# Graph network stack on one core: the order of VectorE's sums in the upper triangle, and the place of the near-diagonal step

## The chip, the cores and the metric

The kernel runs on one core of a Trainium2 chip. The metric is the device time of one execution in microseconds (us). Before the change it was 1927.98, the median of three runs (1926.94 to 1928.78).

## The reference

Four graph layers run one after the other over the same matrix `adj` (8192 x 8192, fp32) and the states `x` (8192 x 64):

```
h = relu(layernorm(x)); x = x + adj @ dropout(h, u)
h = relu(layernorm(x)); x = x + l2norm(relu(concat(h, (adj @ h + h) / (rowsum(adj) + 1)) @ W + b))
h = relu(layernorm(x)); x = x + (D^-1/2 (adj + I) D^-1/2 @ h) @ W      # D = rowsum(adj) + 1
h = relu(layernorm(x)); x = x + concat(h, adj @ h / (rowsum(adj) + 1)) @ W^T
```

Each layer needs one product of the whole matrix with 64 columns, and the row sums of `adj`. A layer's states of a row block exist only when that block's sum over all 8192 columns is done in the layer before.

## The kernel before

**Tiling.** The matrix is cut into 16 x 16 units of 512 x 512. A unit is one load of 1024 KB into one of 12 ring buffers; the diagonal units have two buffers of their own. "Row" means a block of 512 rows. With 64 columns of states as weights a matmul uses half of TensorE's array, and two of them on different halves run side by side; a unit is 4 source tiles of 128 x 512, in fp32 (8 matmul records of one line in the profile).

**Stages.** The matrix doesn't fit in the core's memory, so it is streamed. A first pass (to about 790 us) does layer 0 and the part of layer 1 below the diagonal, and VectorE sums the rows there. The second pass takes the rows from high to low (the upper triangle): a unit there serves layer 1 and layer 2 at once, if the source row's states of both layers are known. It is written in `PAIRS`, two rows at a time: pair 0 is rows (10, 9), pair 1 (8, 7), pair 2 (6, 5), pair 3 (4, 3), pair 4 (2, 1). Row 0 is done in between ("cover") and behind. Then come a head of rows 0 to 3, rows 4 to 15 for layers 2 and 3, and a last stage of single units for layer 3.

**Fours.** In a pair, 2 rows x 2 source rows x 2 layers would be 8 unit products. `four_even` and `four_odd` do them in 7, from combinations of units made by VectorE, each an operation of 128 x 2048:
- `first_form` (L1261): a21 + a22 into `first_sum`, two buffers in turn. It waits for the loads and for the four before last to have used that buffer.
- `third_form` (L1271): a11 - a21 in place of a21.
- `last_forms` (L1281, L1285): first_sum - a11 in place of a11, once TensorE has used a11 in its P1 (`first_taken`); then a12 less this in place of a12, once TensorE has used a12 in its P2 (`second_taken`).

An even four is four steps on TensorE: P2 with P1 (L828, L830), P5 with P4 (L842, L844; needs the first form), P7 with P6 (L852, L854; needs L1281), and P1 of the next four with P3 (L865, L868; needs L1285). An odd four is three: P2 with P4 (L883, L885), P5 with P6 (L890, L892; needs L1281), P7 with P3 (L898, L900; needs L1285).

**The order of a pair** is written out in `PAIR_STEPS`: two covers, fours 0 and 1, the near-diagonal step, four 2, four 3 and plain steps, where pair 1 has fours 0 to 2 only, pair 2 has its one plain step last, and pairs 3 and 4 have plain steps 7 and 6 between fours 2 and 3. Behind the first cover TensorE forms Z (L720) for the higher row of the pair before, behind four 0's first step for the lower one. `near_diagonal` (L905 to L922) multiplies the pair's own near unit for layer 1, and the near unit of the pair before, loaded again, for layer 2 ("behind"); for that it needs the layer-2 states of the higher row of the pair before, and that row is ended by `end_layer_1` on VectorE. `plain_both` (L924) takes one source row for both layers and both rows; the last plain step of a pair needs the layer-2 states of the lower row of the pair before.

**Queues.** Each engine follows its own list in order. SP issues the loads in the order of `loads_in_order`; a load into a ring buffer waits until the unit 12 places before is freed by TensorE, counted in the order of `units_let_go`. VectorE's list for the pairs is the loop at L1487. ScalarE copies P1, makes the square roots of the layer norms and copies the transposed states (`copy_hT`), in an order of its own, in which the copy for row 0 stands between the roots of rows 4 and 3.

Of the kernel before, what the change touches and what calls it, by code (L numbers as in the profile page):

```python
# [205 lines left out]
def gnn_stack(nc, x_in, u_in, stream_in, w1_in, b1_in, w2_in, w3_in, x_out):  # L206
# [6 lines left out]
    with ctx:  # L213
# [6 lines left out]
        def sem(name):  # L220
            return ctx.enter_context(nc.semaphore(name))
# [76 lines left out]
        out_stored = sem("out_stored")  # L298
        states_formed = sem("states_formed")
        late_states_formed = sem("late_states_formed")  # L300
        unit_formed = sem("unit_formed")
        first_taken = sem("first_taken")
        second_taken = sem("second_taken")
# [178 lines left out]
        def _(act):  # L482
# [124 lines left out]
                    if p == len(PAIRS) - 2 and b == PAIRS[p][0]:  # L607
                        copy_hT(1, 0)
            act.wait_ge(*fours_taken(FOURS_BEFORE[-1] - 1))
            act.wait_ge(unit_formed, 4 * FOURS_BEFORE[-1])  # L610
            for r in ADDED[:HEAD]:
                keep_diag(r)

# [50 lines left out]
        def _(pe):  # L664
# [155 lines left out]
            def four_even(p, i, after_first=None, after_second=None):  # L820

                (hi, lo), (s1, s2) = PAIRS[p], FOURS[p][i]
                n, last = FOURS_BEFORE[p] + i, i == len(FOURS[p]) - 1
                a11, a12, a21, a22 = [(2, b, g) for b in (hi, lo) for g in (s1, s2)]
                await_unit(a12, 1)
                await_unit(a11, 1)
                for k in range(TPR):
                    two = nc.tensor.matmul(product("P2"), h[1][:, s2 * TPR + k], source_tile(slot(a12), k),  # L828
                                           start=i == 0 and k == 0, stop=False)
                    one = nc.tensor.matmul(product("P1"), h[1][:, s1 * TPR + k], source_tile(slot(a11), k),  # L830
                                           start=i == 0 and k == 0, stop=i >= len(FOURS[p]) - 2 and k == TPR - 1)
                two.then_inc(second_taken, 1)
                one.then_inc(first_taken, 1)
                if after_first is not None:
                    after_first()
                if i == 0 and p > 0:
                    pe.wait_ge(pair_taken, 3 * p - 2)
                pe.wait_ge(*states_formed_of((s1, s2)))
                pe.wait_ge(unit_formed, 4 * n + 1)
                await_unit(a22, 2)  # L840
                for k in range(TPR):
                    five = nc.tensor.matmul(product("P5"), formed((s1, s2), 1)[:, k], source_tile(first_sum[n % 2], k),  # L842
                                            start=i == 0 and k == 0, stop=last and k == TPR - 1)
                    four = nc.tensor.matmul(product("P4"), formed((s1, s2), 4)[:, k], source_tile(slot(a22), k),  # L844
                                            start=i == 0 and k == 0, stop=False)
                five.then_inc(sum_taken, 1)
                four.then_inc(unit_freed, 1)
                if after_second is not None:
                    after_second()
                pe.wait_ge(unit_formed, 4 * n + 3)  # L850
                for k in range(TPR):
                    seven = nc.tensor.matmul(product("P7"), formed((s1, s2), 3)[:, k], source_tile(slot(a21), k),  # L852
                                             start=i == 0 and k == 0, stop=last and k == TPR - 1)
                    nc.tensor.matmul(product("P6"), formed((s1, s2), 2)[:, k], source_tile(slot(a11), k),  # L854
                                     start=i == 0 and k == 0, stop=last and k == TPR - 1)
                seven.then_inc(unit_freed, 1)
                pe.wait_ge(unit_formed, 4 * n + 4)
                if i == 0 and p > 0:
                    pe.wait_ge(pair_taken, 3 * p - 1)
                if not last:  # L860
                    t1, t2 = FOURS[p][i + 1]
                    await_unit((2, hi, t1), 1)
                for k in range(TPR):
                    if not last:
                        one = nc.tensor.matmul(product("P1 again"), h[1][:, t1 * TPR + k],  # L865
                                               source_tile(slot((2, hi, t1)), k), start=i == 0 and k == 0,
                                               stop=i >= len(FOURS[p]) - 3 and k == TPR - 1)
                    three = nc.tensor.matmul(product("P3"), h[0][:, s2 * TPR + k], source_tile(slot(a12), k),  # L868
                                             start=i == 0 and k == 0, stop=False)
                if not last:  # L870
                    one.then_inc(first_taken, 1)
                three.then_inc(unit_freed, 2)

            def four_odd(p, i):
# [10 lines left out]
                    nc.tensor.matmul(product("P4"), formed((s1, s2), 4)[:, k], source_tile(slot(a22), k),  # L885
                                     start=False, stop=False)
                two.then_inc(second_taken, 1)
                pe.wait_ge(unit_formed, 4 * n + 3)
                for k in range(TPR):
                    five = nc.tensor.matmul(product("P5"), formed((s1, s2), 1)[:, k], source_tile(first_sum[n % 2], k),  # L890
                                            start=False, stop=last and k == TPR - 1)
# [1 line left out]
                                           start=False, stop=last and k == TPR - 1)  # L893
                five.then_inc(sum_taken, 1)
                six.then_inc(unit_freed, 1)
                pe.wait_ge(unit_formed, 4 * n + 4)
                for k in range(TPR):
                    seven = nc.tensor.matmul(product("P7"), formed((s1, s2), 3)[:, k], source_tile(slot(a21), k),  # L898
                                             start=False, stop=last and k == TPR - 1)
# [135 lines left out]
            for p, (hi, lo) in enumerate(PAIRS):  # L1035
                for kind, n in PAIR_STEPS[p]:
# [4 lines left out]
                    elif kind == "four" and n == 0:  # L1041
                        if p == 0:
                            pe.wait_ge(*gathered(1, 11))
                            pe.wait_ge(part_copied, PARTS.index((2, 11)) + 1)
                        four_even(p, 0, after_first=(lambda: finish(1, PAIRS[p - 1][1])) if p else None,
                                  after_second=lambda: turn_own(1, hi))
                        turn_own(1, lo)
                    elif kind == "four" and n % 2 == 0:
                        four_even(p, n)
                        if p == len(PAIRS) - 1:  # L1050
                            turn_own(1, 0)
                    elif kind == "four":
                        four_odd(p, n)
                    elif kind == "near":
                        near_diagonal(p)
                    else:
                        plain_both(p, n)
            cover(COVER_AT_END[0])
            finish(1, PAIRS[-1][0])
# [94 lines left out]
        def _(dve):  # L1154
# [97 lines left out]
            def first_form(p, i):  # L1252
# [6 lines left out]
                if n >= 2:  # L1259
                    dve.wait_ge(*fours_taken(n - 2))  # L1260
                nc.vector.tensor_tensor(first_sum[n % 2][:, :], slot(a21)[:, :], slot(a22)[:, :],  # L1261
                                        ALU.add).then_inc(unit_formed, 1)
                dve.wait_ge(unit_formed, 4 * n + 1)

            def third_form(p, i):

# [3 lines left out]
                dve.wait_ge(*loaded(a11))  # L1270
                nc.vector.tensor_tensor(slot(a21)[:, :], slot(a11)[:, :], slot(a21)[:, :],  # L1271
                                        ALU.subtract).then_inc(unit_formed, 1)
                dve.wait_ge(unit_formed, 4 * n + 2)

            def last_forms(p, i):

# [3 lines left out]
                dve.wait_ge(first_taken, n + 1)  # L1280
                nc.vector.tensor_tensor(slot(a11)[:, :], first_sum[n % 2][:, :], slot(a11)[:, :],  # L1281
                                        ALU.subtract).then_inc(unit_formed, 1)
                dve.wait_ge(unit_formed, 4 * n + 3)
                dve.wait_ge(second_taken, n + 1)
                nc.vector.tensor_tensor(slot(a12)[:, :], slot(a12)[:, :], slot(a11)[:, :],  # L1285
                                        ALU.subtract).then_inc(unit_formed, 1)
                dve.wait_ge(unit_formed, 4 * n + 4)

            def combine_first_layer(p):

# [54 lines left out]
            def begin_layer_1(b):  # L1345
                scaled_z(1, b, deg_clipped_inverse)
# [137 lines left out]
                end_layer_1(b)  # L1484
            scale_own(1, 10)
            scale_own(1, 9)
            for p, (hi, lo) in enumerate(PAIRS):  # L1487
                if p > 0:
                    combine_first_layer(p - 1)
                    begin_layer_1(PAIRS[p - 1][0])  # L1490
                    combine_fifth(p - 1)
                first_form(p, 0)
                if p > 0:
                    combine_high(p - 1)
                third_form(p, 0)
                if p > 0:
                    combine_low(p - 1)
                last_forms(p, 0)
                first_form(p, 1)
                third_form(p, 1)  # L1500
                last_forms(p, 1)
                if p > 0:
                    end_layer_1(PAIRS[p - 1][0], begun=True)
                for n in range(FORMED_BY_GPSIMD, len(SOURCE_PAIRS)):
                    if p > 0 and SOURCE_PAIRS[n][1] == PAIRS[p - 1][0]:
                        form_states(n)
                for i in range(2, len(FOURS[p])):
                    first_form(p, i)
                    third_form(p, i)
                    if i == 2:  # L1510
                        add_behind(p - 1)
                        if p == len(PAIRS) - 1:
                            scale_own(1, 0)
                    last_forms(p, i)
                if p > 0:
                    end_layer_1(PAIRS[p - 1][1])
                if p < len(PAIRS) - 1:
                    for b in PAIRS[p + 1]:
                        scale_own(1, b)
            last = len(PAIRS) - 1  # L1520
            combine_first_layer(last)
            end_layer_1(PAIRS[-1][0])
# [59 lines left out]
```

## Time and profile before

| what | value |
|---|---|
| median of the runs | 1927.98 us (1926.94 to 1928.78) |
| profiled execution: its own time | 1928.73 us |
| its span, first to last instruction | 1926.8 us |
| mean granted TensorE clock | 0.998 |
| TensorE (PE) busy | 1870.4 us, 97% |
| VectorE (DVE) busy | 1065.3 us, 55% |
| ScalarE (ACT) busy | 111.9 us, 6% |
| moved by DMA | 675.63 MB, mean 351 GB/s |

The profile is of one execution; its own time is the span and what lies around it. Times in its views count from the span's start. An idle time in brackets is that of the engine just before an instruction, with what ended it. PEclk is the clock that TensorE was granted, 1.00 being 2.4 GHz.

### The profile page before, as it was taken

The page shows a single profiled execution, that of the slowest core. Times are in us where ns is not written, and L with a number is a line of the kernel's source. Part 1 is how long each engine was busy: PE and PEld are TensorE (multiplying, and loading weights), DVE is VectorE, ACT ScalarE, POOL GpSimd, SP SyncE. Part 2 cuts the span into 40 slices and gives each one's busy share as a digit, 9 for nine tenths or more (in the row PEclk, how much of TensorE's full clock was granted, in tenths as well). Part 3 has the DMA queues.
Part 4 walks back from the last instruction along what each step waited for, and adds up shares of the span by engine and source line. Part 5 has one row for each costly group of instructions (what it writes and reads, how often), then busy time and mean ns, then how long its engine had stood idle before and what let it go on. Part 6 is the DMA issues. An engine that isn't in the chain of part 4 may idle for free.

```text
span 1926.8 us, 19280 instructions
## 1 busy us (share of the span) xinstructions
PE 1870.4 (97%) x7784; PEld 697.8 (36%) x7784; DVE 1065.3 (55%) x1156; ACT 111.9 (6%) x288; POOL 9.6 (0%) x26
## 2 busy tenths in 40 slices
PE   5899999999999999999999999999999999999998
PEld 1233333333333333333333333344444444344343
DVE  8988899999887762867875745321111100110322
ACT  0000000000000001100000001111100000000000
POOL 0000000000000000100000000000000000000000
PEclk9999999999999999999999999999999999999999
DMA  9999999999988884588778787497999889999998
GB/s 386 421 421 421 421 421 421 421 421 411 351 329 321 294 304 172 231 330 355 292 296 323 287 334 278 191 399 288 400 380 366 343 307 422 376 358 415 355 422 341
DMA packets 95894, 675.63 MB, mean 351 GB/s; under 512 B 11200, under 2 KB 13248, under 8 KB 14272
## 3 DMA queue, kind: packets, MB, share of 16 engines
q1 hardware_dynamic: 92880, 672.18, 87.1%
q10 hardware_dynamic: 2928, 2.23, 0.3%
q8 instruction: 63, 1.03, 0.2%
q14 instruction: 23, 0.19, 0.0%
HBM read 672.27 MB, written 2.10 MB: 350 GB/s over the span
## 4 chain that ended last, share of the span: by engine, by line
PE 85%; DMA 8%; DVE 5%; issue 1%; ACT 0%; SPq 0%; DVEq 0%
PE acc L666 43%; PE acc L696 23%; DMA ring<-stream_in 8%; PE Z L720 3%; PE HT L666 2%; PE acc L931 2%; PE DEG L943 2%; PE acc L828 2%; PE acc L852 1%; PE acc L842 1%; PE acc L865 1%; PE acc L883 1%; DVE ring L1285 1%; PE DEG L731 1%; PE DEG L915 1%
## 5 line engine op out<-in xcount | busy, mean ns | idle before, releaser
L666 PE MATMUL acc<-ring,states 128*64 128x512 f32 x3992 | 894.3, 596 | 33.7 <-DMA ring<-stream_in 27.4
L666 PEld LDWEIGHTS acc<-ring,states 128*64 128x64 f32 x3992 | 281.5, 137 | 586.6 <-issue 555.6
L696 PE MATMUL acc<-ring,states 128*128 128x512 f32 x1032 | 453.2, 596 | 2.0 <-DVE states L1225 2.0
L1380 DVE TENSOR_TENSOR row_sum<-row_sum,ring 128x2048 f32<-128x2048 f32 x194 | 444.6, 2292 | 18.5 <-DMA ring<-stream_in 13.5
L696 PEld LDWEIGHTS acc<-ring,states 128*128 128x128 f32 x1032 | 193.5, 191 | 245.1 <-issue 245.1
L1217 DVE TENSOR_TENSOR z_sb<-Z,deg_rsqrt 128x256 f32<-128x256 f32 x16 | 6.8, 424 | 335.3 <-PE Z L720 335.2
L666 PE MATMUL acc<-diag,states 128*64 128x512 f32 x432 | 103.6, 595 | 0.6 <-DMA diag<-stream_in 0.6
L1441 DVE TENSOR_TENSOR y<-acc,y 64x512 f32<-64x512 f32 x36 | 24.6, 683 | 110.8 <-PE acc L666 110.5
L720 PEld LDWEIGHTS Z<-below,y 128*128 128x128 f32 x512 | 62.5, 191 | 51.9 <-issue 18.0
L720 PE MATMUL Z<-below,y 128*128 128x64 f32 x512 | 70.0, 280 | 2.2 <-DVE y L1442 2.2
L1407 DVE TENSOR_TENSOR diag<-diag,ident 128x384 f32<-128x384 f32 x12 | 6.7, 559 | 108.4 <-ACT row_sum L533 108.4
L514 ACT COPY y<-acc 64x512 f32<-64x512 f32 x34 | 19.8, 581 | 748.6 <-PE acc L666 739.9
L1285 DVE TENSOR_TENSOR ring<-ring 128x2048 f32<-128x2048 f32 x17 | 39.0, 2292 | 42.6 <-PE acc L883 42.3
L666 PEld LDWEIGHTS acc<-diag,states 128*64 128x64 f32 x432 | 31.3, 137 | 65.6 <-issue 63.6
L931 PE MATMUL acc<-ring,states 128*64 128x512 f32 x88 | 41.4, 615 | 5.5 <-DVE states L1225 5.5
L666 PE MATMUL HT<-ring,states 128*64 128x512 f32 x168 | 42.6, 595 | 0.0
L1233 DVE TENSOR_TENSOR x<-Z,x 128x256 f32<-128x256 f32 x16 | 6.8, 424 | 63.6 <-PE Z L720 63.3
L933 PE MATMUL acc<-ring,states 128*64 128x512 f32 x88 | 41.5, 616 | 0.0
L1380 DVE TENSOR_TENSOR row_sum<-ring 128x2048 f32<-128x2048 f32 x16 | 36.7, 2292 | 6.7 <-DMA ring<-stream_in 5.8
L943 PE MATMUL DEG<-ring,states 128*64 128x512 f32 x88 | 39.6, 593 | 0.0
L941 PE MATMUL acc<-ring,states 128*64 128x512 f32 x88 | 39.6, 592 | 0.0
L1271 DVE TENSOR_TENSOR ring<-ring 128x2048 f32<-128x2048 f32 x17 | 39.0, 2292 | 0.6
(157 smaller groups left out, 1295.6 us busy)
## 6 DMA issues: line engine op xcount, KB each, us to landing
ring<-stream_in SPq DMA_DIRECT2D x609, 1024.0 KB, 10.3
diag<-stream_in SPq DMA_DIRECT2D x28, 1024.0 KB, 11.6
x<-x_in SPq DMA_DIRECT2D x4, 512.0 KB, 6.7
y<-u_in SPq DMA_DIRECT2D x4, 512.0 KB, 8.5
x_out<-x ACTq DMA_DIRECT2D x16, 128.0 KB, 7.0
below<-w_in ACTq DMA_DIRECT2D x6, 16.0 KB, 5.7
bias<-b_in ACTq DMA_DIRECT2D x1, 32.0 KB, 9.8
```

Of the source, the lines that this page charges most:

```text
L666: return nc.tensor.matmul(half_of(bank, half), h[layer % 2][:, J], moving, start=start, stop=stop)
L696: done = nc.tensor.matmul(acc[bank][:, :], states[:, J * 2 * F:(J + 1) * 2 * F], source_tile(slot(key), k), start=first and k == 0, stop=l ...
L720: mm_z = nc.tensor.matmul(Z[:, t * F:(t + 1) * F], own_y(b)[:, t * P:(t + 1) * P], below[:, layer, :], start=True, stop=True)
L828: two = nc.tensor.matmul(product("P2"), h[1][:, s2 * TPR + k], source_tile(slot(a12), k), start=i == 0 and k == 0, stop=False)
L931: nc.tensor.matmul(product("P2"), h[1][:, J], source_tile(slot((2, hi, g)), k), start=False, stop=last and k == TPR - 1)
L933: done = nc.tensor.matmul(product("P3"), h[0][:, J], source_tile(slot((2, hi, g)), k), start=False, stop=last and k == TPR - 1)
L941: nc.tensor.matmul(product("P4"), h[1][:, J], source_tile(slot((2, lo, g)), k), start=False, stop=last and k == TPR - 1)
L943: done = nc.tensor.matmul(product("plain"), h[0][:, J], source_tile(slot((2, lo, g)), k), start=g == PLAIN[p][0] and k == 0, stop=last and ...
L1271: nc.vector.tensor_tensor(slot(a21)[:, :], slot(a11)[:, :], slot(a21)[:, :], ALU.subtract).then_inc(unit_formed, 1)
L1285: nc.vector.tensor_tensor(slot(a12)[:, :], slot(a12)[:, :], slot(a11)[:, :], ALU.subtract).then_inc(unit_formed, 1)
L1380: nc.vector.tensor_tensor(row_sum[:, :], before, slot(key)[:, :], ALU.add).then_inc(unit_summed, 1 if count > 1 else 2)
L1441: chain(nc.vector.tensor_tensor(own_y(r, 0), half_of(bank, 0), own_y(r, 0), ALU.add))
```

## The change

A semaphore of its own, `sum_formed`, now counts the first forms, so these may be made out of turn; `unit_formed` counts the other three of each four. For pairs 1 to 4 VectorE makes the first and third form of four 0 ahead of combining the pair before, and the first form of four 2 ahead of `last_forms(p, 1)`. In pairs 3 and 4 the lower row of the pair before is ended ahead of four 3's forms. On TensorE the near-diagonal step of pairs 1 to 4 is issued inside four 2, behind its first step, and no longer ahead of it. The order of the loads, the order in which units are counted free, and row 0's own steps are as they were. All calls of `wait_ge` on `unit_formed` go from 4 a four to 3 a four; these are left out below but for two.

```diff
+        sum_formed = sem("sum_formed")
@@ four_even
-                pe.wait_ge(unit_formed, 4 * n + 1)
+                pe.wait_ge(sum_formed, n + 1)
                 await_unit(a22, 2)
...
-                pe.wait_ge(unit_formed, 4 * n + 3)
+                pe.wait_ge(unit_formed, 3 * n + 2)
@@ the steps of a pair on TensorE
                     elif kind == "four" and n % 2 == 0:
-                        four_even(p, n)
+                        four_even(p, n, after_first=lambda: near_diagonal(p))
...
-                    elif kind == "near":
+                    elif kind == "near" and p == 0:
                         near_diagonal(p)
-                    else:
+                    elif kind == "plain":
                         plain_both(p, n)
@@ first_form
-                                        ALU.add).then_inc(unit_formed, 1)
-                dve.wait_ge(unit_formed, 4 * n + 1)
+                                        ALU.add).then_inc(sum_formed, 1)
+                dve.wait_ge(sum_formed, n + 1)
@@ the pairs on VectorE
-            for p, (hi, lo) in enumerate(PAIRS):
-                if p > 0:
-                    combine_first_layer(p - 1)
-                    begin_layer_1(PAIRS[p - 1][0])
-                    combine_fifth(p - 1)
+            first_form(0, 0)
+            third_form(0, 0)
+            last_forms(0, 0)
+            first_form(0, 1)
+            third_form(0, 1)
+            last_forms(0, 1)
+            for p, (before_hi, before_lo) in enumerate(PAIRS[:-1], 1):
+                for b in PAIRS[p]:
+                    scale_own(1, b)
                 first_form(p, 0)
-                if p > 0:
-                    combine_high(p - 1)
                 third_form(p, 0)
-                if p > 0:
-                    combine_low(p - 1)
+                combine_first_layer(p - 1)
+                begin_layer_1(before_hi)
+                combine_fifth(p - 1)
+                combine_high(p - 1)
+                combine_low(p - 1)
                 last_forms(p, 0)
                 first_form(p, 1)
                 third_form(p, 1)
+                first_form(p, 2)
                 last_forms(p, 1)
-                if p > 0:
-                    end_layer_1(PAIRS[p - 1][0], begun=True)
+                end_layer_1(before_hi, begun=True)
                 for n in range(FORMED_BY_GPSIMD, len(SOURCE_PAIRS)):
-                    if p > 0 and SOURCE_PAIRS[n][1] == PAIRS[p - 1][0]:
+                    if SOURCE_PAIRS[n][1] == before_hi:
                         form_states(n)
-                for i in range(2, len(FOURS[p])):
-                    first_form(p, i)
-                    third_form(p, i)
-                    if i == 2:
-                        add_behind(p - 1)
-                        if p == len(PAIRS) - 1:
-                            scale_own(1, 0)
-                    last_forms(p, i)
-                if p > 0:
-                    end_layer_1(PAIRS[p - 1][1])
-                if p < len(PAIRS) - 1:
-                    for b in PAIRS[p + 1]:
-                        scale_own(1, b)
+                third_form(p, 2)
+                last_forms(p, 2)
+                add_behind(p - 1)
+                if p == len(PAIRS) - 1:
+                    scale_own(1, 0)
+                if ("plain", 7) in PAIR_STEPS[p][:-1]:
+                    end_layer_1(before_lo)
+                if len(FOURS[p]) == 4:
+                    first_form(p, 3)
+                    third_form(p, 3)
+                    last_forms(p, 3)
+                if ("plain", 7) not in PAIR_STEPS[p][:-1]:
+                    end_layer_1(before_lo)
```

## Rows read from the trace of the kernel before

**Rows 1.** The page, part 1: busy, instructions; part 5: busy, mean ns | idle before, releaser.
```profile
PE 1870.4 (97%) x7784; PEld 697.8 (36%) x7784; DVE 1065.3 (55%) x1156; ACT 111.9 (6%) x288; POOL 9.6 (0%) x26
...
L696 PE MATMUL acc<-ring,states 128*128 128x512 f32 x1032 | 453.2, 596 | 2.0 <-DVE states L1225 2.0
```
**Rows 2.** Waits of PE, 843 to 1215 us: in total, times, longest.
```profile
PE DEG L915 <- DVE states L1225: 7.5, 4, 1.9
PE acc L931 <- DVE states L1225: 5.5, 3, 2.2
```
**Rows 3.** Timeline of PE: start, us, engine, line; idle before in brackets.
```profile
898.17 0.61 PE L931 MATMUL acc<-ring,states 128*64 128x512 f32 x1 [1.13 <-DVE states L1225]
...
971.36 0.61 PE L931 MATMUL acc<-ring,states 128*64 128x512 f32 x1 [2.19 <-DVE states L1225]
...
1005.77 0.59 PE L890 MATMUL acc<-row_sum,diag 128*64 128x512 f32 x1
...
1012.21 0.59 PE L898 MATMUL acc<-ring,diag 128*64 128x512 f32 x1
...
1014.68 0.61 PE L915 MATMUL DEG<-ring,states 128*64 128x512 f32 x1 [1.87 <-DVE states L1225]
...
1058.29 0.99 PE L931 MATMUL acc<-ring,states 128*64 128x512 f32 x1 [2.19 <-DVE states L1225]
...
1187.09 5.37 PE L696 MATMUL acc<-ring,states 128*128 128x512 f32 x8 [1.95 <-DVE states L1225]
```
**Rows 4.** Timeline of DVE in the pairs, same columns.
```profile
856.12 0.68 DVE L1322 TENSOR_TENSOR y<-DEG,pair_sums 64x512 f32<-64x512 f32 x1 [0.32 <-PE Z L720]
...
881.27 2.29 DVE L1261 TENSOR_TENSOR row_sum<-ring 128x2048 f32<-128x2048 f32 x1
...
885.93 0.68 DVE L1330 TENSOR_TENSOR y<-DEG,y 64x512 f32<-64x512 f32 x1
...
891.51 0.42 DVE L1217 TENSOR_TENSOR z_sb<-Z,deg_clipped_inverse 128x256 f32<-128x256 f32 x1
...
897.60 0.42 DVE L1225 SCALAR_TENSOR_TENSOR states<-centred,inverse 128x256 f32<-128x256 f32 x1
...
978.50 0.68 DVE L1294 TENSOR_TENSOR y<-acc,y 64x512 f32<-64x512 f32 x1 [6.49 <-PE DEG L943]
...
998.83 2.29 DVE L1271 TENSOR_TENSOR ring<-ring 128x2048 f32<-128x2048 f32 x1
1002.09 2.29 DVE L1281 TENSOR_TENSOR ring<-row_sum,ring 128x2048 f32<-128x2048 f32 x1 [0.97 <-PE acc L865]
1006.05 2.29 DVE L1285 TENSOR_TENSOR ring<-ring 128x2048 f32<-128x2048 f32 x1 [1.66 <-PE acc L883]
...
1014.00 0.42 DVE L1225 SCALAR_TENSOR_TENSOR states<-centred,inverse 128x256 f32<-128x256 f32 x1
...
1067.13 0.68 DVE L1294 TENSOR_TENSOR y<-acc,y 64x512 f32<-64x512 f32 x1 [8.19 <-PE DEG L943]
```
**Rows 5.** Timeline of ACT in pair 4, same columns.
```profile
1121.10 0.74 ACT L521 COPY y<-HT 64x256 f32<-64x256 f32 x2 [18.91 <-PE HT L763]
```
**Rows 6.** SP's loads: the one issued at 877.8, then the one at 883.3.
```profile
DMA to landing us min/median/max: 4.8/4.8/4.8
...
DMA to landing us min/median/max: 10.7/10.7/10.7
```
**Rows 7.** A window in pair 3: us, PE busy, PEclk, DMA share, GB/s.
```profile
1059.00:1060.00 1.00, 1.00 (x6) 0.50 1.12 475
```
**Rows 8.** Windows ahead of and in the last stage, same columns.
```profile
1790.00:1800.00 10.00, 10.00 (x44) 1.00 0.71 233
...
1870.00:1880.00 10.00, 10.00 (x54) 1.00 1.02 425
```
**Rows 9.** Waits of PE, then of SP, from 1215 us on.
```profile
PE acc L666 <- DMA ring<-stream_in: 1.3, 3, 0.6
...
SPq L432 <- PE acc L696: 314.2, 102, 4.2
```

## What the change will do

> **What bounds the kernel now.** I read the page first: TensorE is busy 97% of the span [rows 1], so only its idle time, its clock and its own work can move the end. Then its waits in the stretch of pairs 1 to 4: four waits of the near-diagonal step (L915) and three of a plain step (L931), all on a state that VectorE writes at L1225 [rows 2]. Then the timelines, to see what stands ahead of those states.
>
> The idle time in that view runs from the modelled end of a matmul. Matmuls of one half last 0.59 and start 0.43 apart (15 starts lie between the first L890 at 1005.77 and the last L898 at 1012.21, 6.44 / 15) [rows 3], so a wait costs 0.16 more than its idle time. In pair 3 the last L898 starts at 1012.21, the next step was due at 1012.64 and starts at 1014.68: 2.04 lost for 1.87 idle. The four near-diagonal waits (7.5 idle, about 1.87 each) are worth 2.04 each; the plain ones 1.29 in pair 1 (idle 1.13), 2.35 in pair 2 and 2.35 in pair 3 (idle 2.19 both).
>
> The one in pair 3 costs more. Behind it the granted clock is 0.50, the 1.2 GHz level [rows 7]. From the state's end to the first combine, with one plain step on TensorE between them, VectorE idles 8.19 there and 6.49 behind the equal wait of pair 2 [rows 4]: the low clock cost 1.70. The wait before 1187.09, in row 0's steps behind the pairs, has the same sequel: eight matmuls take 5.37 [rows 3], where 8 x 453.2 / 1032 = 3.51 is usual [rows 1]. The change doesn't touch that wait.
>
> **The change, part by part.**
>
> *Near-diagonal step behind the third four's first step.* The state it waits for ends a chain in pair 3 of L1281 at 1002.09, L1285 at 1006.05 (held by the second four's first step), the end of layer 1, and L1225, which ends at 1014.42 [rows 4]. The third four's first step needs neither that state nor a sum, only loaded units and layer-1 states. It takes eight starts of 0.43, 3.43 in all, so the near step comes due at 1012.64 + 3.43 = 1016.07, 1.4 after the state is ready. All four waits go. What could be late next is the third step of that four, which needs L1281: with its sum made before, VectorE does L1271 and L1281 in 2 x 2.33 behind the state (two such forms take 4.66 from 881.27 to 885.93, [rows 4]), ready at about 1019.1, and TensorE asks for it two more steps on, at 1022.9. Spare 3.8.
>
> The two near-diagonal units come free one step later, and SP takes loads in order, so everything behind them may be issued 3.43 later. In pair 2's case the load that waits for the freed unit was issued at 883.3 and took 10.7 to land, at 894.0, where the one issued at 877.8 took 4.8 [rows 6]; it was mostly queued, and up to 5 of delay vanishes in that queue. VectorE asks for it only after the state at 898.02. I take 0; the ends are 0 and 3.43 a pair.
>
> *First and third forms ahead of combining.* These are 2 x 2.33 = 4.66 of VectorE work moved in front of the pair's end, where it idles 6.49 (pair 2's end) and 8.19 (pair 3's) [rows 4]; pair 1's forms have no layer end in their way. They fit with 1.8 to spare. Behind the pair's end nothing gets earlier by it: combine_low waits for Z until 856.12 in pair 1 [rows 4], after which come L1281 and L1285 as now. So this part gains 0 by itself and costs 0. If the cover is gone, each us beyond the spare delays the first combine; TensorE has one cover step of 3.51 [rows 1] before it needs the third of these adds (3 x 0.72 = 2.2, 0.68 each in [rows 4] and 0.04 to the next), so 1.3 more is free.
>
> *The third four's sum ahead of last_forms(p, 1).* L1271 starts at 998.83, the sum would run from 1001.16, L1281 from 1003.49 to 1005.78 in place of 1002.09 to 1004.38. Today VectorE is idle there, 0.97 before L1281 and 1.66 before L1285 [rows 4], 2.63 together, so the sum's 2.33 fits and L1285 still starts at 1006.05: the state is no later. But TensorE's second step of the second four starts at 1005.77 [rows 3], and from VectorE's end to a matmul's start it takes 0.15 (898.02 to 898.17) to 0.26 (1014.42 to 1014.68). It would start at 1005.93 to 1006.04: a new wait of 0.16 to 0.27, in all four pairs. No trace shows this wait itself; bounded below by 0 (a hidden start) and above by the next smallest wait of this kind, 1.29. The instants are known to 0.01, so I take 0.2, 0.8 in all.
>
> *End of the lower row.* Pair 1: behind its new states VectorE starts L1271 at 881.27 in place of the sum, does three forms (6.99) and L1330 (0.72) by 888.98, then the layer's end, 6.51 from 891.51 to 898.02: state at 895.49, TensorE at 895.64. TensorE would be ready at 898.17 - 1.29 - 2.04 + 0.2 = 895.04. The plain step starts at 895.64 and 0.6 of its wait stays: the gain of pair 1, near step and new wait included, is 2.53.
> Pair 2: the layer's end stays behind the fourth four's last form, which waits for that four's first step. Both engines keep their distance from there, and the 2.35 stays. Gain 2.04 - 0.2 = 1.84.
> Pair 3: the layer's end now lies under the third four and two plain steps (4 x 3.43 = 13.7), so the 2.35 and the 1.70 of low clock go. Gain 1.84 + 2.35 + 1.70 = 5.89.
> Pair 4: no plain wait today. The layer's end asks ScalarE for a root, behind its copy of row 0's turned states, which starts at 1121.10 and takes 0.74, after the third four [rows 5]. VectorE stops there until about 1121.9, then needs 4.5 to the state and 3 x 2.33 for the fourth four's forms: 1133.4 by today's times. TensorE asks for them two plain steps and one more behind about 1121.0, at 1138.1. Spare 4.7, cost 0. Gain 1.84.
>
> **Sum.** 2.53 + 1.84 + 5.89 + 1.84 = 12.10. Of this 10.4 is idle time and 1.70 is clock. The profiled execution took 1928.73 (span 1926.8 and 1.93 around it), 0.75 over the median of the runs; since the sum holds a clock loss seen in it, I take it from its own time: 1928.73 - 12.10 = 1916.6. Does it reach the end? Loads behind the pairs are issued when TensorE frees units (SP waits 314.2 for L696 after 1215), TensorE waits for DMA 1.3 in all [rows 9], and just ahead of the last stage the DMA share falls to 0.71 [rows 8], so the ring is full when that stage starts and its loads shift with TensorE.
>
> **The rivals.**
>
> *The clock falls elsewhere.* Of two equal waits of 2.19 [rows 3] one was followed by a fall, the other not. Pair 2's wait stays and may cost 1.70; row 0's may not: 1918.3 or 1914.9, both at once give no difference. The Trainium skill (TensorE: Matmul & The Clock Gate, Part 1) says that the observation runs freely and is not tied to the program, which would make this a matter of chance in each execution; by it 1918.3 is as fair as 1916.6, and the two equal waits with different sequels agree.
>
> *The pairs' ends keep their waits*, because VectorE is late with something the timelines hide (the root behind the copy, add_behind waiting for the later near step). Then pair 3 keeps its 4.05 and pair 1 its 0.7: 1921.4. Against it: the spares of 3.8 and 4.7.
>
> *Given back in the last stage.* There the DMA share is 1.02 [rows 8]; if it sets the pace from before row 0's steps, nothing is left: 1928.7. Against it: the 0.71 ahead of that stage and the short DMA waits [rows 8, 9].
>
> *Slower: combining waits behind the hoisted forms.* If the loads of a pair's first four landed only at the pair's end, both forms would run behind it: 4.66 less 1.3 free, 3.36 in four pairs, 13.4 against 12.1 gained. From 0.7 later than that it is measurably slower: 1932.8. It decides only if the loads come much later than now; pair 2's landed at 894.0, before VectorE can ask.
>
> **How the numbers follow.** 0.56 for the forecast, 0.20 for the clock, 0.10 for the kept waits, 0.09 for given back, 0.05 for slower. Low end: no new wait (0.8), no fall behind row 0's wait (1.7) and the 0.75 to the median: 1913.3, widened to 1912.8. High end: kept waits, 1921.4, widened to 1921.8; new waits near their upper bound would reach it too. Beyond that lie the last two cases, 0.14. A measurement tells 0.2% (3.9 us) from no change: faster 0.86, same 0.09, slower 0.05.
>
> **What would show it.** L915 has no wait, L890 four short ones near 0.05 to 0.1 idle, L931 one below 0.6 in pair 1 and one near 2.2 in pair 2, none in pair 3; the wait behind 1166 stands some 12 us earlier. VectorE shows L1261 and L1271 before the first combine. Wrong would be: waits of L720 or L842 at a pair's start, L890 waits over 0.5, or DMA waits of TensorE near the end.

## The result and the profile after

The changed kernel takes 1918.49 us (median of 4 runs, 1917.7 to 1920.65) against 1927.46 (4 runs) for the kernel before: ratio 0.9949, 95% interval 0.9936 to 0.9961, 9.0 us faster. The profiled execution took 1920.65, span 1918.7, which is 8.1 under the 1928.73 of the profiled execution before. The forecast was 1916.6, a gain of 12.1.

The page of the changed kernel, part 1 (the lines of code named here are one higher than before):

```profile
PE 1868.0 (97%) x7784; PEld 692.7 (36%) x7784; DVE 1065.1 (56%) x1156; ACT 112.1 (6%) x288; POOL 9.6 (0%) x26
```

TensorE's waits in the changed kernel, 843 to 1215 us (total, times, longest). They answer to [rows 2]:

```profile
PE acc L866 <- issue: 3.0, 2, 1.8
PE acc L932 <- DVE states L1226: 2.8, 2, 2.2
PE acc L697 <- DVE states L1226: 2.0, 1, 2.0
```

The near-diagonal step (now L916) is gone from the list. Of the three plain waits two are left. New is L866, the fourth step of a four, whose releaser the view doesn't find. The timeline of PE shows where these are (idle time before in brackets, [rows 3] before):

```profile
896.56 0.61 PE L932 MATMUL acc<-ring,states 128*64 128x512 f32 x1 [0.56 <-DVE states L1226]
...
967.78 0.95 PE L932 MATMUL acc<-ring,states 128*64 128x512 f32 x1 [2.21 <-DVE states L1226]
...
1026.60 0.61 PE L866 MATMUL acc<-ring,states 128*64 128x512 f32 x1 [1.83 <-issue]
...
1110.56 0.61 PE L866 MATMUL acc<-ring,states 128*64 128x512 f32 x1 [1.21 <-issue]
...
1180.61 3.67 PE L697 MATMUL acc<-ring,states 128*128 128x512 f32 x8 [1.95 <-DVE states L1226]
```

The waits of 0.56 and 2.21 in pairs 1 and 2 are as forecast. Behind the second the clock fell (first matmul 0.95 long); behind the last, row 0's, it did not: 3.67 for eight matmuls where before it was 5.37. L866 multiplies the first unit of the next four's higher row, in pair 3 unit (4, 9), in pair 4 unit (2, 9). SP's view of the loads of these two, in the changed kernel:

```profile
L433 SPq DMA_DIRECT2D ring<-stream_in x1: 327/327/327, 1017.9 to 1017.9; - x1
...
DMA to landing us min/median/max: 8.6/8.6/8.6
...
L433 SPq DMA_DIRECT2D ring<-stream_in x1: 328/328/328, 1102.5 to 1102.5; - x1
...
DMA to landing us min/median/max: 8.0/8.0/8.0
```

1017.9 + 8.6 = 1026.5, and TensorE starts at 1026.60; 1102.5 + 8.0 = 1110.5, and it starts at 1110.56. "issue" hid a DMA. The load of the same unit in pair 3 before the change, by SP's view:

```profile
L432 SPq DMA_DIRECT2D ring<-stream_in x1: 328/328/328, 1018.3 to 1018.3; - x1
...
DMA to landing us min/median/max: 9.3/9.3/9.3
```

and the timeline of PE:

```profile
1028.44 0.59 PE L865 MATMUL acc<-ring,states 128*64 128x512 f32 x1
```

It landed at 1027.6 and was read at 1028.44: 0.8 spare. What changed is the distance from the issue, when the near step frees the buffer, to the read. Before, three steps of TensorE lay between them, 10.1 (1018.3 to 1028.44). In the changed kernel there are two: the read was due at 1024.6 (1026.60 less the 1.83 idle and 0.16), 6.7 behind the issue at 1017.9. The load took 0.7 less there (8.6 for 9.3), so one step of 3.43 less the spare of 0.8 and this 0.7 is a loss of 1.9, as measured.

In pair 4 the load of (2, 9) took 9.2 from 1107.0 before and was read at 1117.06, a spare of 0.9. It took 1.2 less in the changed kernel (8.0), which gives a loss of 1.3; measured are 1.21 idle and 0.16.

Cutting the span at each start of combining gives a time for each pair. VectorE's first combine, before:

```profile
843.49 0.68 DVE L1294 TENSOR_TENSOR y<-acc,y 64x512 f32<-64x512 f32 x1 [11.44 <-PE DEG L943]
905.31 0.68 DVE L1294 TENSOR_TENSOR y<-acc,y 64x512 f32<-64x512 f32 x1 [6.49 <-PE DEG L943]
...
1165.97 0.68 DVE L1294 TENSOR_TENSOR y<-acc,y 64x512 f32<-64x512 f32 x1 [18.66 <-PE DEG L943]
```

and after:

```profile
844.49 0.68 DVE L1295 TENSOR_TENSOR y<-acc,y 64x512 f32<-64x512 f32 x1 [6.71 <-PE DEG L944]
903.77 0.68 DVE L1295 TENSOR_TENSOR y<-acc,y 64x512 f32<-64x512 f32 x1 [2.03 <-PE DEG L944]
976.69 0.68 DVE L1295 TENSOR_TENSOR y<-acc,y 64x512 f32<-64x512 f32 x1 [3.73 <-PE DEG L944]
1061.28 0.68 DVE L1295 TENSOR_TENSOR y<-acc,y 64x512 f32<-64x512 f32 x1 [6.17 <-PE DEG L944]
1159.49 0.68 DVE L1295 TENSOR_TENSOR y<-acc,y 64x512 f32<-64x512 f32 x1 [25.20 <-PE DEG L944]
```

The idle times show the forms made ahead: 11.44 becomes 6.71. The table has the differences of such rows for every kernel of this study (e8 to e10 are second profiles); a star marks a pair that holds a fall of the clock, 1.70 long.

| kernel | pair 1 | pair 2 | pair 3 | pair 4 | start to pair 1 | behind pair 4 |
|---|---|---|---|---|---|---|
| before | 61.82 | 73.19 | 88.63* | 98.84 | 843.49 | 760.8* |
| e8, before again | 61.82 | 74.89* | 88.62* | 98.84 | 844.83 | 760.7* |
| after | 59.28 | 72.92* | 84.59 | 98.21 | 844.49 | 759.2 |
| e0, after again | 59.28 | 72.92* | 84.70 | 98.20 | 844.59 | 758.8 |
| e1 | 62.53 | 74.88* | 84.52 | 98.77 | 844.12 | 759.2 |
| e2 | 61.61 | 72.25 | 86.11 | 98.02 | 843.87 | 759.2 |
| e3 | 59.28 | 71.23 | 82.53 | 96.79 | 843.55 | 758.3 |
| e9, e3 again | 59.29 | 72.93* | 82.54 | 96.78 | 843.84 | 760.4* |
| e4 | 61.83 | 73.18 | 84.52 | 98.84 | 843.38 | 758.6 |
| e5 | 61.82 | 73.18 | 88.61* | 98.77 | 843.60 | 760.4* |
| e6 | 58.57 | 68.80 | 82.53 | 96.79 | 845.21 | 761.1* |
| e10, e6 again | 58.57 | 68.80 | 82.53 | 96.79 | 844.14 | 760.5* |
| e7 | 59.28 | 71.22 | 82.54 | 96.85 | 843.62 | 760.4* |

The column "start to pair 1" is the start of combining itself, counted from the span's start. Between executions of one kernel a pair repeats within about 0.1 apart from the falls, while the unchanged part ahead of pair 1 varies by 1.3 (843.49 and 844.83 in the kernel before).

### The profile page after: what moved, and what is told of

Same layout as the page of the kernel before. It is cut to its first block, busy times and chain, and to the rows that moved or that the text cites. A ratio compares the mean times of both kernels' runs of the same rounds, so it can differ in the third digit from the quotient of the medians.

```text
span 1918.7 us, 19280 instructions
## 1 busy us (share of the span) xinstructions
PE 1868.0 (97%) x7784; PEld 692.7 (36%) x7784; DVE 1065.1 (56%) x1156; ACT 112.1 (6%) x288; POOL 9.6 (0%) x26
## 4 chain that ended last, share of the span: by engine, by line
PE 89%; DMA 7%; DVE 3%; issue 1%; SPq 0%; ACT 0%; DVEq 0%
PE acc L667 44%; PE acc L697 23%; DMA ring<-stream_in 7%; PE Z L721 3%; PE HT L667 2%; PE acc L932 2%; PE DEG L944 2%; PE acc L829 2%; PE acc L843 2%; PE acc L853 1%; PE acc L866 1%; PE acc L884 1%; PE acc L899 1%; PE acc L891 1%; PE DEG L732 1%; PE DEG L916 1%
```

## The experiments

All were timed beside the kernel before (4 to 11 runs of each kernel), apart from the three second profiles. The median of the kernel before on those chips was 1928.5 to 1928.9.

**e0, the changed kernel again.** 

> The changed kernel as it is, beside the others on one chip. 1918.5 (9.0 under before). TensorE's first P1 matmul of four 3 (inside four 2) waits 1.8 in pair 3 and 1.2 in pair 4, as in the first profile.

1919.85, ratio 0.9952 (0.9939 to 0.9964). The L866 waits are there again, 1.94 and 1.19.

**e1, the near step put back; e3, one load moved.** Two theories on L866: the load came late, because SP could issue it only when the near step had freed its buffer; or a form of VectorE held it.

```diff
# e1
-                        four_even(p, n, after_first=lambda: near_diagonal(p))
+                        four_even(p, n)
...
-                    elif kind == "near" and p == 0:
+                    elif kind == "near":
# e3, in step_loads and in units_let_go
+        if p >= 3 and n == 3:
+            return [(2, hi, s1), (2, lo, s1), (2, lo, s2), (2, hi, s2)]
...
-            at = PLACE[2, lo, s1]
+            at = min(PLACE[2, lo, s1], PLACE[2, hi, s1])
```

> The changed kernel with the near-diagonal step put back ahead of four 2; VectorE's order stays changed. Theory (loads): the waits of P1 in pairs 3 and 4 come from the load of four 3's unit (4, 9) or (2, 9), which SP can't issue before the near step has freed its units; with the near step ahead they vanish (3.4 won), the four near waits of 2.04 return (8.2 lost), pair 1's plain wait vanishes (0.7 won): 4.1 over the changed kernel, about 1922.6, less 1.7 where the clock falls once less. Rival (forms): those waits are for VectorE, whose order changed, and then they stay: about 1926.

> The changed kernel, with the load of four 3's first unit of the higher row issued ahead of the two of the lower row, in pairs 3 and 4 alone: two places earlier, where it waits for units that the second four frees. Theory (loads): it lands 5 us earlier, both waits of P1 go, 3.4 won: about 1915.1. Rival (forms): nothing moves, 1918.5. A second rival (DMA bandwidth): the lower row's loads land later in its place and VectorE's forms of four 3 hold TensorE, 1917 to 1919.

e3 takes 1914.27, ratio 0.9925 (0.9911 to 0.9938), and neither pair has a wait on L866's step. VectorE's order is that of the changed kernel, so the form theory falls, and the lower row's later loads cost nothing. In pair 3 the unit is issued at 1009.3, 35.2 behind the pair's start where it was 41.2 in the changed kernel's first profile. SP's loads in e3:

```profile
L435 SPq DMA_DIRECT2D ring<-stream_in x1: 430/430/430, 1009.3 to 1009.3; - x1
...
DMA to landing us min/median/max: 8.9/8.9/8.9
```

It lands at 1018.2. The step that reads it, in e3's timeline of PE, holds this matmul and no wait:

```profile
1021.97 0.59 PE L868 MATMUL acc<-ring,states 128*64 128x512 f32 x1
```

Against e0, pairs 3 and 4 are 2.17 and 1.41 shorter: 3.6 for the expected 3.4. The medians lie 5.6 apart, which is more. In the profiles the rest is falls of the clock and the part ahead of pair 1 (e9, the same kernel, took 1917.76 once); that the same holds for the other runs is not shown.

e1 takes 1925.33, ratio 0.9982 (0.9973 to 0.9991), where 1922.6 was expected. L866 waits no more, which agrees. But the near waits came back at 1.76 and pair 1 didn't win its 0.7: it lost 3.25 against after in place of the 1.3 expected there. Two waits of TensorE stand in pair 1 of e1:

```profile
880.22 0.61 PE L916 MATMUL DEG<-ring,states 128*64 128x512 f32 x1 [1.76 <-DVE states L1226]
899.44 0.61 PE L932 MATMUL acc<-ring,states 128*64 128x512 f32 x1 [1.84 <-DVE states L1226]
```

and VectorE, in e1, shows why the second is there:

```profile
881.84 2.29 DVE L1272 TENSOR_TENSOR ring<-ring 128x2048 f32<-128x2048 f32 x1
...
887.42 2.29 DVE L1282 TENSOR_TENSOR ring<-row_sum,ring 128x2048 f32<-128x2048 f32 x1 [3.29 <-PE acc L831]
```

L1282 waits 3.29 for the third four's first step, which with the near step ahead ends 3.4 later, and the sum's 2.33 taken out of VectorE's chain only makes this wait longer. So in pair 1 the early sum is worth something only when the near step stands behind.

**e2, only the near step moved; e4, only the lower row's end; e5, only the forms.** The kernel before with one part of the change each.

```diff
# e2
-                        four_even(p, n)
+                        four_even(p, n, after_first=lambda: near_diagonal(p))
# e4, ahead of the forms of four 3; from the end of pairs 3 and 4 it is taken away
+                    if i == 3 and p >= 3:
+                        end_layer_1(PAIRS[p - 1][1])
# e5: the changed kernel with e1's lines, and
                 third_form(p, 2)
-                last_forms(p, 2)
                 add_behind(p - 1)
...
+                last_forms(p, 2)
...
+                end_layer_1(before_lo)      # at the end of every pair, in place of both calls
```

> The kernel before, with nothing changed but the near-diagonal step, which stands behind four 2's first step. If the parts of the change were independent, it would win the 8.2 of the near waits less the 3.4 of the new load waits: 4.8, about 1922.7. Theory: in pair 1 VectorE's chain from the higher row's states over three forms and add_behind to the lower row's states is what bounds, and TensorE only waits longer at the plain step, so pair 1 wins nothing: 2.0 (pair 2) + 0.05 (pair 3) + 0.7 (pair 4) = 2.8, about 1924.7.

> The kernel before, with nothing changed but the place of the lower row's end in pairs 3 and 4, ahead of four 3's forms. Theory: pair 3's plain wait of 2.35 goes and nothing else, 1925.1, or 1923.4 where the clock fell behind that wait. The near waits (4 x 1.87 idle) stay. Rival: VectorE's stop at the root in pair 4 holds four 3's forms: slower than before.

> The kernel before, with nothing changed but the forms: first and third of four 0 ahead of combining, the sum of four 2 ahead of last_forms(p, 1). Theory: the near waits stay, and the sum's 2.33 leaves the chain from the higher to the lower row's states in pair 1, whose plain wait of 1.29 goes: 1926.2. The forms ahead of combining win 0. Rival: hoisting alone makes the states earlier, near waits shorter by 1 or more each: 1922 or less.

e2: 1925.34, ratio 0.9980 (0.9971 to 0.9989), 3.2 under before where the theory said 2.8 and independent parts 4.8. Pair 1 gives 0.2 in place of 2.5. The near waits are gone in it, and TensorE has these instead:

```profile
889.38 0.64 PE L852 MATMUL acc<-ring,diag 128*64 128x512 f32 x1 [0.90 <-DVE ring L1281]
898.34 0.61 PE L931 MATMUL acc<-ring,states 128*64 128x512 f32 x1 [1.88 <-DVE states L1225]
...
1026.82 0.61 PE L865 MATMUL acc<-ring,states 128*64 128x512 f32 x1 [1.05 <-DVE row_sum L1261]
```

Without the early sum L1281 comes 2.33 later, and VectorE's chain from the higher to the lower row's states sets the plain step. The third line is the load wait of pair 3: the view names L1261, but TensorE's step doesn't wait for this form, and by SP's view the load was issued at 1018.9 and took 7.8, so it landed at 1026.7. In pair 4 it is 0.76. So the near step alone brings the load waits, with VectorE's order as it was.

e4: 1923.14, ratio 0.9973 (0.9962 to 0.9984). Pair 3 is 4.11 shorter, the 2.41 of the wait and the 1.70 of the fall behind it; no other pair moves, and the stop at the root costs nothing. The medians lie 5.4 apart, 1.2 more than pair 3 gives; row 0's wait had no fall behind it in e4's profile and had one in both of the kernel before.

e5: 1928.63, ratio 1.0002 (0.9993 to 1.0011): nothing, where 1.3 was expected in pair 1. The forms alone gain 0, for the reason that e1 showed. In the kernel before, VectorE's timeline has the wait that decides it:

```profile
886.86 2.29 DVE L1281 TENSOR_TENSOR ring<-row_sum,ring 128x2048 f32<-128x2048 f32 x1 [0.25 <-PE acc L830]
```

In e5 this form (now L1282) waits 2.58 and starts at the same distance from the pair's start, 43.30 for 43.37.

By the medians the three alone give 3.2 + 5.4 - 0.1 = 8.4, with falls of the clock mixed in, and together 9.0. By the pairs, the stars taken off at 1.70 each, it is 2.8 + 2.4 + 0.1 = 5.3 against 7.5: the sum lacks 2.3 in pair 1 and 1.0 in pair 2, where the near step and the early sum need each other, and has 1.2 too much in pairs 3 and 4, where the load waits are longer in the whole change.

**e7, forms where they were.** The changed kernel with e3's load, but the first and third form of four 0 not ahead of combining:

```diff
-                first_form(p, 0)
-                third_form(p, 0)
                 combine_first_layer(p - 1)
                 begin_layer_1(before_hi)
                 combine_fifth(p - 1)
+                first_form(p, 0)
                 combine_high(p - 1)
+                third_form(p, 0)
                 combine_low(p - 1)
```

> The run with four 3's unit first, but the first and third form of four 0 made where they were before, among the steps of combining. Theory: they win nothing, since behind them combine_low waits for Z anyway: the same as that run, pairs of 59.3, 71.2, 82.5 and 96.8 from combine to combine. Rival (the hoist matters with the near step moved): pair's first steps wait for L1262 or the states come up to 4.7 later, and 1 to 2 a pair are lost, 1918 to 1922.

1915.63, ratio 0.9932 (0.9918 to 0.9945), an interval that overlaps with e3's, and the pairs are those of e3 within 0.06. This part wins nothing.

**e6, fewer waits.** e3's load, and VectorE's idle times around four 3 in pair 2 filled:

```diff
+                    if p == 2:
+                        begin_layer_1(before_lo)
+                        norm_asked(before_lo)       # bias, squares, sum, root asked
...
+                    last_forms(p, 3, between=(lambda: norm_taken(before_lo)) if p == 2 else None)
+                if p == 2:
+                    states_after_norm(before_lo)
# pair 1
+                if p == 1:
+                    end_layer_1(before_lo)
                 add_behind(p - 1)
```

> As the run with that unit first, and in pair 2 the lower row's layer end is begun in VectorE's idle times around four 3's L1282, and in pair 1 it stands ahead of add_behind. Theory: of the 6.5 of the layer end some 2.9 leave the chain behind L1286, so pair 2's wait of 2.35 goes, and pair 1's 0.7 too: 3.1 under the run before, about 1912.0, and no wait is left in the pairs behind which the clock could fall (up to 1.7 more in an execution where it fell there). Rival: the inserted small operations delay L1282 past TensorE's second step (0.4 spare) and the wait only moves to L891: about 1914 to 1915.

1912.37, ratio 0.9916 (0.9903 to 0.9930), 16.5 under before, the lowest median of all. The intervals of e6 and e3 overlap and the medians lie 1.9 apart, so the times alone don't tell the two; the pairs do: pair 1 is 0.71 and pair 2 2.43 shorter than in e3, 3.1 as expected, in both profiles of e6. In e6's window over all pairs TensorE has no idle time (us, PE busy, PEclk, DMA share, GB/s):

```profile
843.00:1170.00 327.00, 327.00 (x1432) 1.00 0.82 333
```

**e8 to e10, does the instant decide a fall?** In the first profiles of before, e4 and e5 the wait near 971 had no fall behind it, and those at 1058.3 and 1187.1 (before, e5) each had one.

> The kernel before, a second profile. Theory (the instant decides): TensorE's waits at 1058.3 and 1187.1 from the span's start are again followed by the clock at 0.50, that at 971.4 is not. Rival (chance in each execution): the fall stands behind other waits than in the first profile, or none.

> The kernel with four 3's unit first, a second profile. Theory (the instant decides): no fall behind the waits near 966.8 and 1174.5, as in its first profile. Rival (chance): a fall behind one of them in one of these looks.

> The kernel with fewer waits, a second profile. Theory (the instant decides): the one long wait left, near 1173.0, is again followed by a fall, eight matmuls of 5.37. Rival (chance): they may take 3.67.

e8 has a fall behind all three, also at 972.71. e9 has two where e3 had none. e10 has its one fall again (eight matmuls of 5.37), which both answers allow. In pair 2 of e9 it comes 1.3 into the plain step:

```profile
967.15 0.61 PE L934 MATMUL acc<-ring,states 128*64 128x512 f32 x1 [2.21 <-DVE states L1228]
...
968.47 1.06 PE L934 MATMUL acc<-ring,states 128*64 128x512 f32 x1
```

So which wait is followed by a fall differs between executions of one kernel. This doesn't settle the theory in its strict form, for in e8 and e9 the waits ended 0.3 to 3.0 later than in the first profiles (972.71 for 971.36), and where two kernels' waits ended at the same instant (before and e5 at 971.4, 1058.3 and 1187.1) the sequels were equal. Against it stands row 0's wait in two kernels, which ended 0.15 apart, with opposite sequels. In e3:

```profile
1174.49 3.67 PE L699 MATMUL acc<-ring,states 128*128 128x512 f32 x8 [1.94 <-DVE states L1228]
```

and in e7:

```profile
1174.64 5.37 PE L699 MATMUL acc<-ring,states 128*128 128x512 f32 x8 [1.95 <-DVE states L1228]
```

Chance in each execution fits all 13 profiles, but what decides a fall is not shown. Over all 13 profiles here a fall stands behind 15 of the 29 waits of 1.94 to 2.21 and behind none of the shorter ones in the pairs.

## Why the prediction was right or wrong

The measured time lies in the range, 1.9 over the value, on the side of the high end. That it is only 1.9 is in part luck. I subtracted the gain from the time of the profiled execution, 1928.73, which lies 1.3 over the median of the four runs before. Median against median the gain is 9.0 for 12.1, and profile against profile 8.1: 2.9 of idle time is missing, and the part ahead of pair 1, which the change doesn't touch, happened to take 1.0 more (844.49 for 843.49).

- *The four near waits go*: right, all four, and L1282 was in time. e2 confirms that the move alone does it; there a new wait of 0.90 for L1281 leaves 0.94 of the 2.04 in pair 2.
- *The new wait of L890*: too large. The timeline of DVE in pair 1 of the changed kernel:

```profile
869.40 2.29 DVE L1282 TENSOR_TENSOR ring<-row_totals,ring 128x2048 f32<-128x2048 f32 x1
```

and that of PE:

```profile
871.75 0.64 PE L891 MATMUL acc<-row_totals,diag 128*64 128x512 f32 x1
```

The step (now L891) starts 0.06 behind VectorE's end, and its first matmul lasts 0.64 in place of 0.59; no idle time shows. I had put 0.2 a pair; from the pair's start it begins at 27.26 and began at 27.27 (870.76) before, so at most the 0.05 of the longer matmul is lost, and 0.6 of the 0.8 never was.
- *Pair 1*: 2.53 forecast, 2.54 measured. *Pair 2*: 1.84 forecast, 1.97 measured with the fall taken off (73.19 less 72.92 - 1.70); its plain wait stays, 2.21 as said.
- *Pairs 3 and 4*: 5.89 and 1.84 forecast, 4.04 and 0.63 measured. This is the step that failed: "The two near-diagonal units come free one step later [...] I take 0; the ends are 0 and 3.43 a pair". I looked at one load, the one issued at 883.3 behind pair 1's near step; it brings a unit of pair 2's first four, which VectorE asks for only behind the state at 898.02. In pairs 3 and 4 four plain units stand between, and the first load that waits for the near step's buffer is four 3's first unit of the higher row, which TensorE reads in four 2, before the plain steps. Its spare was 0.8 in pair 3 and 0.9 in pair 4, in the trace of before, less than the 3.43 that the prediction itself gave as the upper end, and I had not set the load beside its reader. It cost 1.99 and 1.37 (idle plus 0.16), 3.36 in all; e3 gives back 3.6. The idle time won fell short by 2.9 (7.5 for 10.4), less than this error, since the waits of L891 were smaller.
- *Clock*: the 1.70 behind pair 3's wait went, with the wait (e4 shows both together). In the profiled execution a fall came in pair 2, which had none, and row 0's went. That is the rival "the clock falls elsewhere" with both halves at once, which gives no difference, as it said. The Trainium skill (TensorE: Matmul & The Clock Gate, Part 1) has the observation run free of the program. The profiles agree with it: 2 and 3 falls in the two of before, 0 and 2 in those of e3 and e9.
- *Hoisted forms gain 0*: right (e5, e7).
- *It reaches the end*: right; behind pair 4 it is 760.8 and 759.2, apart by one fall.
- *Pair 4's stop at the root*: there as said and free. In the changed kernel VectorE shows it, and the idle time of 5.16 ahead of four 3's last form, so the forms were not late for TensorE:

```profile
1115.62 0.18 DVE L1361 RECIPROCAL inverse<-rooted 128x4 f32<-128x4 f32 x1 [8.43 <-ACT rooted L499]
...
1132.00 2.29 DVE L1286 TENSOR_TENSOR ring<-ring 128x2048 f32<-128x2048 f32 x1 [5.16 <-PE acc L884]
```

My expectations for e1 and e5 missed by the same thing, the 0.25 that L1281 waited for L830 in pair 1 before the change: a sum taken out of VectorE's chain was no gain as long as TensorE's step that releases L1281 stood behind the near step.

## What to carry to other kernels

When a step is moved past others, list for each buffer that it frees the one load that waits for it, and set that load's landing beside the first reader of the unit, in every repetition of the loop whose order differs; one repetition says nothing on the others. A form taken out of one engine's chain pays only if the other engine's release of the next one is not later: look for a small idle time in the chain that names that release, here 0.25. Here the early sum paid only together with the move of the near step, and the forms ahead of combining could be left out.

## What the runs showed of the hardware

A wait of 1.94 to 2.21 of a busy TensorE was followed by 1.2 GHz in about half of the cases (15 of 29), for a loss of 1.70 each. None of the shorter waits in the pairs, up to 1.88, had one. The fall came at once or up to 1.3 into the work behind the wait (e9). It is one cause of the spread between executions of a kernel: the two profiled executions of e3's kernel, with no fall and with two, lie 4.1 apart (1913.66 and 1917.76), and 3.4 of it is falls. A matmul that must wait for VectorE started as little as 0.06 behind it (871.69 to 871.75 in after), against 0.15 and 0.26 after longer waits.
